# Longer warming products, x tile 0 ahead of W, and the ids product moved behind label 0's work

## The chip, the cores and the metric

The kernel runs on one core of a Trainium2 chip. The metric is the time of one execution on the device in microseconds (us), as the median of several runs. Beside it stands a profile of one further execution: a page and a trace, whose times count from the start of the span (the stretch from the first to the last instruction).

## The reference

Two linear layers with residuals act on `x` of shape 64 x 32 x 512 (batch, sequence, features), all in float32. Cut to what matters:

```python
x = x + einsum('bct,bcd->bdt', x, W0[cond])          # a 32 x 32 mix of each batch's rows, W0 chosen by cond
base  = einsum('bsi,oi->bso', x, W)                  # W is 512 x 512
low   = einsum('bsi,bir->bsr', x, lora_A[label])     # label in 0..2 here, 5 labels of A, rank 32
delta = einsum('bsr,or->bso', low, lora_B_w) * 0.5
x = x + (base + delta)
```

## The kernel before

**The tiling.** A tile is 128 rows of x (four batches of 32), a pair is two tiles; there are 16 tiles in 8 pairs. Since both layers are linear, the kernel applies the second one first: u = x times M, where M = (identity + W transposed + A of label 0 times B), and mixes the rows of u by a block-diagonal matrix (identity + W0 chosen by `cond`) afterwards. Labels other than 0 are handled by the difference of their A to A of label 0 (`a_diff`), whose product with x (`p_low`) is masked by `keep`, folded (`p_fold`) and multiplied with B (`delta_tile`). To keep float32 accuracy with the rounded type fp32r, an operand is split in two, hi (rounded by ScalarE) and lo (the remainder, by VectorE): `xt_hi`/`xt_lo`, `m_hi`/`m_lo`, `ad_hi`/`ad_lo` and so on.

**The five instruction streams.** Each engine has its own list of instructions, written out by hand and worked off strictly in order; semaphores join them. SyncE (SP) issues the loads of W, of x and the stores; ScalarE (ACT) issues three loads first, then copies and rounds; VectorE (DVE) makes remainders and masks; GpSimd (POOL) makes the identity, the indices, the differences of A and the gathers of W0; TensorE (PE) transposes and multiplies.

**The start on TensorE** (lines 637 to 700), in order: seven warming products of a 128 x 128 float32 tile of ones with itself into `p_low` (L639), whose result nothing uses; the transposes of B and A of label 0 (L643); the transposes of W, two quarters (L616); the transposes of x tile 0 into `p_low` (L632); the ids product (`spread_ids`, L650), which spreads `cond` and `label` over 128 partitions into `p_fold`; `lora_half(0)` (L622), which adds A times B to the left half of M; the other two quarters of W; `lora_half(1)`; the transposes of x tile 1 into `p_fold`, behind a wait for the copy of the ids; then `main_tile` for tiles 0 and 1, left half, `main_tile` for tile 0, right half; `low_pair(0)` (L573, L574, and with a wait for `ad_lo` L578); `main_tile` for tile 1, right half; `low_pair(1)`, `fold_pair` (L594, L595); and from there a loop over pairs.

**What hangs on the ids.** DVE copies the ids product out of PSUM (L477, `ids_all`, semaphore `s_ids_sb`). POOL waits for it before it makes the row numbers `w0_row` (L267, four instructions), the mask `keep` (L270), `a_diff` (L276), the gathers of W0 for tiles 0 and 1 (L252) and `ad_lo` (L285), in that order. ACT makes `ad_hi` (L337) from `a_diff`.

**Order on DVE** at the start: memsets; `bw_rep` and `a_rep` (L449 to L457); the identity added to two diagonal blocks of W (L464); `fold_parts`, `fold_to`; the ids to fp32r (L475); the ids' copy (L477), the remainder of x tile 0 (L403), the remainders of the left half of M (L483), and so on. POOL adds the identity to the other two diagonal blocks (L248). Order on ACT: `b_stack` (L327), `a_stack` (L329), x tile 0 rounded (L302), `m_hi` left half (L323), x tile 1 rounded.

Of the kernel before, what the change touches and what calls it, by code (L numbers as in the profile page):

```python
# [27 lines left out]
F32 = mybir.dt.float32  # L28
F32R = mybir.dt.float32r
# [4 lines left out]
P = 128  # L34


def conditioned_lora_kernel(nc, x, cond, label, W0, W, A, Bw, out):
    B, S, T = x.shape
# [6 lines left out]
    OC = O // P  # L45
    Q = P // R
    ROWS = 2 * P
    WARM = 7
    H = O // 2
    W_ORDER = (1, 0, 3, 2)  # L50
    LOOPS = PAIRS // 2 - 1
# [12 lines left out]
    with ExitStack() as ctx:  # L64
        def sb(name, shape, dt=F32):
            return ctx.enter_context(nc.sbuf_tensor(name, shape, dt))
# [5 lines left out]
            return ctx.enter_context(nc.semaphore(name))  # L72


        warm = sb("warm", [P, P])
        ident = sb("ident", [P, P])
        fold_id = sb("fold_id", [P, R])
        fold_parts = sb("fold_parts", [P, 2, 2, 2, R])
# [5 lines left out]
        ids_i = sb("ids_i", [1, 2, B], I32)  # L84
        ids_r = sb("ids_r", [1, 2, B], F32R)
        ones_r = sb("ones_r", [1, P], F32R)
        ids_all = sb("ids_all", [P, 2, B])
        w0_row = sb("w0_row", [P, TILES], I32)
        keep = sb("keep", [P, B])
        w_sb = sb("w_sb", [P, OC, T])  # L90
        a_sb = sb("a_sb", [P, NL, C, R])
        bw_sb = sb("bw_sb", [P, OC, R])
# [29 lines left out]
        p_y = [ps(f"p_y{i}", [P, O]) for i in range(2)]  # L122
        p_low = ps("p_low", [P, O])
        p_fold = ps("p_fold", [P, O])


        s_cond_in = sem("s_cond_in")
# [60 lines left out]
        @blk.sync  # L188
        def _(sp):

            def load(p, slot):

                for q in range(Q):
                    sp.dma_start(x_sb[R * q:R * (q + 1), slot].rearrange("s u b j -> s (u b) j"),
                                 x_pair[p, q]).then_inc(s_x_in[slot], 16)

            def store(p):
                sp.wait_ge(s_y_copied, 2 * p + 2)
                sp.dma_start(out_pair[p], y_sb[:, bass.ds(2 * p, 2)]).then_inc(s_y_out, 16)

            sp.dma_start(bw_sb[:], Bw.rearrange("(o p) r -> p o r", p=P)).then_inc(s_bw_in, 16)
            sp.dma_start(w_sb[:, 0], W[0:P, :]).then_inc(s_w_in[0], 16)
            sp.dma_start(x_rows[:, 0], x_tile[0]).then_inc(s_rows_in[0], 16)
            sp.dma_start(ids_i[:, 0], cond.unsqueeze(0)).then_inc(s_cond_in, 16)
            sp.dma_start(ids_i[:, 1], label.unsqueeze(0)).then_inc(s_label_in, 16)
            sp.dma_start(w_sb[:, 2], W[2 * P:3 * P, :]).then_inc(s_w_in[2], 16)
            sp.dma_start(x_rows[:, 1], x_tile[1]).then_inc(s_rows_in[1], 16)
            sp.dma_start(a_sb[:, 1:NL].rearrange("p l c r -> p l (c r)"), A_cols[:, 1:NL]).then_inc(s_a_in, 16)
            load(1, 1)
            load(2, 0)  # L210

            with sp.Fori(0, LOOPS - 1) as g:
                for slot in (1, 0):
                    sp.wait_ge(s_xt, 2 * (2 * g + 2 - slot))
                    load(2 * g + 4 - slot, slot)
                    store(2 * g + 1 - slot)
            sp.wait_ge(s_xt, 2 * (PAIRS - 3))
            load(PAIRS - 1, 1)
            store(PAIRS - 4)
            store(PAIRS - 3)  # L220
            store(PAIRS - 2)
            sp.wait_ge(s_y_copied, TILES - 1)
            sp.dma_start(out_tile[TILES - 2], y_sb[:, TILES - 2]).then_inc(s_y_out, 16)
            sp.wait_ge(s_last, 2)
            sp.dma_start(out_tile[TILES - 1], y_sb[:, TILES - 1]).then_inc(s_y_out, 16)
            sp.wait_ge(s_y_out, 16 * (PAIRS + 1))
# [65 lines left out]

        @blk.scalar
        def _(act):
            act.dma_start(a_sb[:, 0].rearrange("p c r -> p (c r)"), A_cols[:, 0]).then_inc(s_a0_in, 16)
            act.dma_start(w_sb[:, 1], W[P:2 * P, :]).then_inc(s_w_in[1], 16)
            act.dma_start(w_sb[:, 3], W[3 * P:4 * P, :]).then_inc(s_w_in[3], 16)

            def split_rows(u, bank):

                act.wait_ge(s_rows_t, u + 1)
                nc.scalar.activation(xt_hi[:, 0, :, P * u:P * (u + 1)],  # L302
                                     bank[:].rearrange("p (c r) -> p c r", c=C), COPY).then_inc(s_xhi, 1)
# [16 lines left out]
            def split_m(half, b):  # L320
# [2 lines left out]
                nc.scalar.activation(m_hi[:, 2 * b:2 * b + 2, halves[half]],  # L323
                                     p_u[2 * half + b][:].rearrange("p (c o) -> p c o", c=2), COPY).then_inc(s_mhi, 1)

            act.wait_ge(s_bT, 1)
            nc.scalar.activation(b_stack[:], p_y[0][:], COPY, scale=0.5).then_inc(s_b_stack, 1)  # L327
            act.wait_ge(s_aT, 1)
            nc.scalar.activation(a_stack[:], p_y[1][:], COPY).then_inc(s_a_stack, 1)  # L329
            split_rows(0, p_low)  # L330
            split_m(0, 0)
            split_m(0, 1)
            split_rows(1, p_fold)
# [59 lines left out]
        def _(dve):  # L393
# [5 lines left out]
            def split_rows(u, bank):  # L399

                dve.wait_ge(s_xhi, u + 1)
                cols = slice(P * u, P * (u + 1))
                nc.vector.tensor_tensor(xt_lo[:, 0, :, cols], bank[:].rearrange("p (c r) -> p c r", c=C),  # L403
                                        xt_hi[:, 0, :, cols].bitcast(F32), ALU.subtract).then_inc(s_xlo, 1)
# [26 lines left out]
                                        ALU.subtract).then_inc(s_keptlo, 1)  # L431


            nc.vector.memset(warm[:], 1.0).then_inc(s_warm, 1)
            for j in range(BT):
                nc.vector.memset(group[R * j:R * (j + 1)], float(j)).then_inc(s_group, 1)
            nc.vector.memset(block[:], 0.0).then_inc(s_group, 1)
# [2 lines left out]
            for j in range(BT):  # L440
# [1 line left out]
            dve.wait_ge(s_pool, 1)  # L442
            nc.vector.scalar_tensor_tensor(row_of[:], group[:], -float(R), p_num[:], ALU.mult,
                                           ALU.add).then_inc(s_row_of, 1)
            nc.vector.tensor_copy(ones_r[:], warm[0:1, :]).then_inc(s_ids, 1)

            dve.wait_ge(s_bw_in, 16)
            bw_two = bw_sb[:].unsqueeze(2).broadcast_to([P, OC, 2, R])
# [12 lines left out]
            for o in W_ORDER[:2]:  # L461
                dve.wait_ge(s_w_in[o], 16)
                w_diag = w_sb[:, o, P * o:P * (o + 1)]
                nc.vector.tensor_tensor(w_diag, w_diag, ident[:], ALU.add).then_inc(s_diag, 1)  # L464

            dve.wait_ge(s_pool, 4 + Q)
            for part in range(2):
                nc.vector.tensor_copy(fold_parts[:, part, :, part],
# [4 lines left out]
            dve.wait_ge(s_cond_in, 16)  # L473
            dve.wait_ge(s_label_in, 16)
            nc.vector.tensor_copy(ids_r[:], ids_i[:]).then_inc(s_ids, 1)  # L475
            dve.wait_ge(s_ids_all, 1)
            nc.vector.tensor_copy(ids_all[:].rearrange("p u b -> p (u b)"), p_fold[:, 0:2 * B]).then_inc(s_ids_sb, 1)  # L477

            def split_m(half, b):

                dve.wait_ge(s_mhi, 2 * half + b + 1)
                two, cols = slice(2 * b, 2 * b + 2), halves[half]
                nc.vector.tensor_tensor(m_lo[:, two, cols], p_u[2 * half + b][:].rearrange("p (c o) -> p c o", c=2),  # L483
                                        m_hi[:, two, cols].bitcast(F32), ALU.subtract).then_inc(s_mlo, 1)

            split_rows(0, p_low)
            split_m(0, 0)
            split_m(0, 1)
            split_rows(1, p_fold)
            split_m(1, 0)  # L490
            split_m(1, 1)
# [75 lines left out]
        def _(pe):  # L567
# [13 lines left out]
            def main_tile(bank, slot, u, cols=slice(0, O), half=None):  # L581

                to = bank[:, cols]
                rows = slice(P * u, P * (u + 1))
                for c in range(C):
                    if half is not None:
                        pe.wait_ge(s_mlo, 2 * half + c // 2 + 1)
                    mm(to, xt_hi[:, slot, c, rows], m_hi[:, c, cols], start=(c == 0 and half != 1), stop=False)  # L588
                    mm(to, xt_hi[:, slot, c, rows], m_lo[:, c, cols], start=False, stop=False)  # L589
                    mm(to, xt_lo[:, slot, c, rows], m_hi[:, c, cols], start=False, stop=False)  # L590
# [36 lines left out]
            def transpose_rows(u, bank):  # L627

                pe.wait_ge(s_rows_in[u], 16)
                rows_t = x_rows[:, u].rearrange("p (t c) -> p c t", c=C)  # L630
                for c in range(C):
                    last = mm(bank[:, P * c:P * (c + 1)], rows_t[:, c], ident[:], start=(c == 0), stop=(c == C - 1),  # L632
                              is_transpose=True)
                last.then_inc(s_rows_t, 1)
# [1 line left out]

            pe.wait_ge(s_warm, 1)
            for i in range(WARM):
                mm(p_low[:, 0:P], warm[:], warm[:], start=True, stop=True)  # L639

            def transpose_groups(bank, source):
                for c in range(C):
# [4 lines left out]
            def spread_ids():  # L647

                pe.wait_ge(s_ids, 2)
                mm(p_fold[:, 0:2 * B], ones_r[:], ids_r[:].rearrange("p u b -> p (u b)"), start=True,  # L650
                   stop=True).then_inc(s_ids_all, 1)

            pe.wait_ge(s_pool, 3)
            pe.wait_ge(s_rep, 2)
            transpose_groups(p_y[0], bw_rep).then_inc(s_bT, 1)
            pe.wait_ge(s_rep, 4)
# [2 lines left out]
            transpose_w(0)  # L659
            pe.wait_ge(s_diag, 2)  # L660
            transpose_w(1)
            transpose_rows(0, p_low)
            spread_ids()
            pe.wait_ge(s_b_stack, 1)
            pe.wait_ge(s_a_stack, 1)
            lora_half(0)
# [2 lines left out]
            pe.wait_ge(s_diag_right, 2)  # L669
            transpose_w(3)  # L670
            lora_half(1)
            pe.wait_ge(s_ids_sb, 1)
            transpose_rows(1, p_fold)

            pe.wait_ge(s_xlo, 1)
            main_tile(p_y[0], 0, 0, left, half=0)
            pe.wait_ge(s_xlo, 2)
            main_tile(p_y[1], 0, 1, left, half=0)
            main_tile(p_y[0], 0, 0, right, half=1)
            pe.wait_ge(s_adhi, 1)  # L680
# [76 lines left out]
```

## Time and profile before

| what | value |
|---|---|
| median of 3 runs | 88.50 us (88.23 to 88.61) |
| the profiled execution's own time | 88.51 us |
| its span | 86.7 us |
| PE busy | 82.6 us, 95% of the span |
| DVE busy | 55.8 us, 64% |
| ACT busy | 39.6 us, 46% |
| POOL busy | 23.3 us, 27% |

A difference of two kernels is read on the executions' times; the span leaves out 1.8 us around the instructions. The chain of waits goes back from the last instruction to what released each one; its pieces begin where the piece before them ends, so a piece on PE can start some 0.1 to 0.2 us later than the record of the same product in the timeline, whose records overlap.

### The profile page before, as it was taken

The page shows a single profiled execution, that of the slowest core. Times are in us where ns is not written, and L with a number is a line of the kernel's source. Part 1 is how long each engine was busy: PE and PEld are TensorE (multiplying, and loading weights), DVE is VectorE, ACT ScalarE, POOL GpSimd, SP SyncE. Part 2 cuts the span into 40 slices and gives each one's busy share as a digit, 9 for nine tenths or more (in the row PEclk, how much of TensorE's full clock was granted, in tenths as well). Part 3 has the DMA queues.
Part 4 walks back from the last instruction along what each step waited for, and adds up shares of the span by engine and source line. Part 5 has one row for each costly group of instructions (what it writes and reads, how often), then busy time and mean ns, then how long its engine had stood idle before and what let it go on. Part 6 is the DMA issues. An engine that isn't in the chain of part 4 may idle for free.

```text
span 86.7 us, 1411 instructions
## 1 busy us (share of the span) xinstructions
PE 82.6 (95%) x463; PEld 72.9 (84%) x463; DVE 55.8 (64%) x117; ACT 39.6 (46%) x80; POOL 23.3 (27%) x37
## 2 busy tenths in 40 slices
PE   5999999999999999999999999999999999999950
PEld 5999999998888988898889888988898888889940
DVE  3672879975984696469744984499249933731550
ACT  0544492233547573457255616551754273415440
POOL 5322798977008001800170008000710000000000
PEclk9999999999999999999999999999999999999999
DMA  1999990370000494646037502770250015000606
GB/s 27 314 350 310 199 188 19 83 178 12 8 0 8 147 267 81 203 126 176 2 140 230 134 0 83 230 186 0 80 177 0 0 50 192 8 0 3 239 14 228
DMA packets 12393, 10.16 MB, mean 117 GB/s; under 512 B 1508, under 2 KB 9572, under 8 KB 12388
## 3 DMA queue, kind: packets, MB, share of 16 engines
q1 hardware_dynamic: 11444, 9.24, 38.1%
q10 hardware_dynamic: 432, 0.59, 2.1%
q0 software_dynamic: 512, 0.26, 1.7%
q8 instruction: 3, 0.05, 0.3%
q14 instruction: 2, 0.02, 0.1%
HBM read 5.90 MB, written 4.19 MB: 116 GB/s over the span
## 4 chain that ended last, share of the span: by engine, by line
PE 95%; DVE 1%; issue 0%
PE p_u L588 15%; PE p_u L589 15%; PE p_u L590 15%; PE p_low L573 5%; PE p_low L578 5%; PE p_low L574 4%; PE p_low L639 4%; PE p_u L599 4%; PE p_y L605 4%; PE p_y L606 4%; PE p_y L608 4%; PE p_u L616 3%; PE p_y L588 2%; PE p_y L589 2%; PE p_y L590 2%; PE p_y L643 2%
## 5 line engine op out<-in xcount | busy, mean ns | idle before, releaser
L252 POOL DMA_INDIRECT w_sel<-in_L_cond_weights,w_row x16 | 16.3, 1019 | 33.4 <-DVE diag L499 30.3
L588 PE MATMUL p_u<-m_hi,xt_hi 128*128 128x512 f32 (+1 forms) x60 | 22.6, 377 | 0.0
L589 PE MATMUL p_u<-m_lo,xt_hi 128*128 128x512 f32 (+1 forms) x60 | 22.6, 377 | 0.0
L590 PE MATMUL p_u<-m_hi,xt_lo 128*128 128x512 f32 (+1 forms) x60 | 22.5, 375 | 0.0
L410 DVE TENSOR_TENSOR xt_lo<-xt,xt_hi 128x512 fp32r<-128x512 f32 x14 | 10.1, 728 | 8.4 <-ACT xt_hi L308 8.4
L396 DVE STREAM_TRANSPOSE xt<-x_sb 128x512 f32<-128x512 f32 x14 | 15.1, 1091 | 0.0
L416 DVE TENSOR_TENSOR u_lo<-p_u,u_hi 128x512 fp32r<-128x512 f32 (+1 forms) x15 | 9.3, 652 | 8.9 <-ACT u_hi L313 8.8
L318 ACT ACTIVATE y_sb<-p_y 128x512 f32 (+1 forms) x13 | 7.7, 591 | 12.2 <-PE p_y L608 12.2
L590 PEld LDWEIGHTS p_u<-m_hi,xt_lo 128*128 128x128 f32 x60 | 11.3, 188 | 2.1
L588 PEld LDWEIGHTS p_u<-m_hi,xt_hi 128*128 128x128 f32 x60 | 11.3, 188 | 1.9
L589 PEld LDWEIGHTS p_u<-m_lo,xt_hi 128*128 128x128 f32 x60 | 11.3, 188 | 1.8
L313 ACT ACTIVATE u_hi<-p_u 128x512 fp32r<-128x512 f32 (+1 forms) x15 | 7.8, 568 | 8.7 <-PE p_u L599 8.7
L308 ACT ACTIVATE xt_hi<-xt 128x512 fp32r<-128x512 f32 x14 | 8.8, 632 | 3.9 <-DVE xt L396 1.9
L573 PE MATMUL p_low<-xt_hi,ad_hi 128*128 128x256 f32 x32 | 8.0, 284 | 0.0
L574 PE MATMUL p_low<-xt_lo,ad_hi 128*128 128x256 f32 x32 | 8.0, 283 | 0.0
L341 ACT ACTIVATE kept_hi<-kept 128x256 fp32r<-128x256 f32 x8 | 3.3, 418 | 7.2 <-DVE kept L423 7.2
L573 PEld LDWEIGHTS p_low<-xt_hi,ad_hi 128*128 128x128 f32 x32 | 6.1, 190 | 0.4 <-issue 0.2
L574 PEld LDWEIGHTS p_low<-xt_lo,ad_hi 128*128 128x128 f32 x32 | 6.1, 191 | 0.2
L506 DVE TENSOR_TENSOR diag_lo<-diag,diag_hi 128x256 fp32r<-128x256 f32 x8 | 3.3, 418 | 3.2 <-ACT diag_hi L349 3.2
L605 PE MATMUL p_y<-u_hi,diag_hi 128*128 128x512 f32 (+1 forms) x14 | 5.4, 385 | 0.0
L606 PE MATMUL p_y<-u_hi,diag_lo 128*128 128x512 f32 (+1 forms) x14 | 5.4, 385 | 0.0
L608 PE MATMUL p_y<-u_lo,diag_hi 128*128 128x512 f32 (+1 forms) x14 | 5.3, 381 | 0.0
(92 smaller groups left out, 126.7 us busy)
## 6 DMA issues: line engine op xcount, KB each, us to landing
x_sb<-in_x SPq DMA_DIRECT2D x28, 128.0 KB
out<-y_sb SPq DMA_DIRECT2D x7, 512.0 KB, 3.2
w_sb<-in_L_cond_W ACTq DMA_DIRECT2D x2, 256.0 KB, 3.9
w_sb<-in_L_cond_W SPq DMA_DIRECT2D x2, 256.0 KB, 3.8
x_rows<-in_x SPq DMA_DIRECT2D x2, 256.0 KB, 4.5
out<-y_sb SPq DMA_DIRECT2D x2, 256.0 KB, 2.1
a_sb<-in_L_cond_lora_A SPq DMA_DIRECT2D x1, 256.0 KB, 5.3
w_sel<-in_L_cond_weights,w_row POOLq DMA_INDIRECT x16
```

Source lines behind the costliest of these rows:

```text
L252: nc.gpsimd.indirect_dma_start(out=w0_sel[:, t, :], out_offset=None, in_=W0_rows, in_offset=bass.IndirectOffsetOnAxis(ap=w0_row[:, t:t + 1 ...
L308: nc.scalar.activation(xt_hi[:, slot, :, P * u:P * (u + 1)], xt[:, u], COPY).then_inc(s_xhi, 1)
L396: nc.vector.transpose(xt[:, u].rearrange("p c (b s) -> p c b s", s=S), x_sb[:, slot, u].rearrange("p b (i c) -> p c b i", c=C)).then_inc(s ...
L410: nc.vector.tensor_tensor(xt_lo[:, slot, :, cols], xt[:, u], xt_hi[:, slot, :, cols].bitcast(F32), ALU.subtract).then_inc(s_xlo, 1)
L416: nc.vector.tensor_tensor(u_lo[:, u, cols], bank[:, cols], u_hi[:, u, cols].bitcast(F32), ALU.subtract).then_inc(s_ulo, 1)
L573: mm(p_low[:, 0:ROWS], ad_hi[:, c], xt_hi[:, slot, c], start=(c == 0), stop=False)
L574: mm(p_low[:, 0:ROWS], ad_hi[:, c], xt_lo[:, slot, c], start=False, stop=False)
L588: mm(to, xt_hi[:, slot, c, rows], m_hi[:, c, cols], start=(c == 0 and half != 1), stop=False)
L589: mm(to, xt_hi[:, slot, c, rows], m_lo[:, c, cols], start=False, stop=False)
L590: mm(to, xt_lo[:, slot, c, rows], m_hi[:, c, cols], start=False, stop=False)
L605: mm(to[:, cols], diag_hi[:, slot, u], u_hi[:, u, cols], start=True, stop=False)
L606: mm(to[:, cols], diag_lo[:, slot, u], u_hi[:, u, cols], start=False, stop=False)
```

## The change

The seven warming products become six, of the rounded type and 512 columns wide each. SP issues x tile 0 first and then the four quarters of W in the order in which they are used; Bw, A of label 0 and the ids go on ACT's queue. The transposes of x tile 0 stand in front of B's on PE, and their rounding and remainder stand correspondingly ahead on ACT and DVE. The ids product moves from in front of `lora_half(0)` to behind `lora_half(1)` and writes to `p_y[1]` instead of `p_fold`; its copy on DVE moves behind the remainders of the left half of M; PE waits for that copy before `p_y[1]` is next written.

```diff
-    WARM = 7
+    WARM = 6
-        warm = sb("warm", [P, P])
+        warm = sb("warm", [P, P], F32R)
# SP
-            sp.dma_start(bw_sb[:], Bw.rearrange("(o p) r -> p o r", p=P)).then_inc(s_bw_in, 16)
-            sp.dma_start(w_sb[:, 0], W[0:P, :]).then_inc(s_w_in[0], 16)
             sp.dma_start(x_rows[:, 0], x_tile[0]).then_inc(s_rows_in[0], 16)
-            sp.dma_start(ids_i[:, 0], cond.unsqueeze(0)).then_inc(s_cond_in, 16)
-            sp.dma_start(ids_i[:, 1], label.unsqueeze(0)).then_inc(s_label_in, 16)
-            sp.dma_start(w_sb[:, 2], W[2 * P:3 * P, :]).then_inc(s_w_in[2], 16)
+            for o in W_ORDER:
+                sp.dma_start(w_sb[:, o], W[P * o:P * (o + 1), :]).then_inc(s_w_in[o], 16)
# ACT
+            act.dma_start(bw_sb[:], Bw.rearrange("(o p) r -> p o r", p=P)).then_inc(s_bw_in, 16)
             act.dma_start(a_sb[:, 0].rearrange("p c r -> p (c r)"), A_cols[:, 0]).then_inc(s_a0_in, 16)
-            act.dma_start(w_sb[:, 1], W[P:2 * P, :]).then_inc(s_w_in[1], 16)
-            act.dma_start(w_sb[:, 3], W[3 * P:4 * P, :]).then_inc(s_w_in[3], 16)
+            act.dma_start(ids_i[:, 0], cond.unsqueeze(0)).then_inc(s_cond_in, 16)
+            act.dma_start(ids_i[:, 1], label.unsqueeze(0)).then_inc(s_label_in, 16)
+            split_rows(0, p_low)
             act.wait_ge(s_bT, 1)
...
-            split_rows(0, p_low)
             split_m(0, 0)
# DVE
+            split_rows(0, p_low)
             dve.wait_ge(s_pool, 4 + Q)
...
-            dve.wait_ge(s_ids_all, 1)
-            nc.vector.tensor_copy(ids_all[:]..., p_fold[:, 0:2 * B]).then_inc(s_ids_sb, 1)
-            split_rows(0, p_low)
             split_m(0, 0)
             split_m(0, 1)
+            dve.wait_ge(s_ids_all, 1)
+            nc.vector.tensor_copy(ids_all[:]..., p_y[1][:, 0:2 * B]).then_inc(s_ids_sb, 1)
             split_rows(1, p_fold)
# PE
-                mm(p_low[:, 0:P], warm[:], warm[:], start=True, stop=True)
+                mm(p_low[:], warm[:], warm[:].unsqueeze(1).broadcast_to([P, 4, P]), start=True, stop=True)
-                mm(p_fold[:, 0:2 * B], ones_r[:], ids_r[:]..., start=True,
+                mm(p_y[1][:, 0:2 * B], ones_r[:], ids_r[:]..., start=True,
             pe.wait_ge(s_pool, 3)
+            transpose_rows(0, p_low)
             pe.wait_ge(s_rep, 2)
...
-            transpose_rows(0, p_low)
-            spread_ids()
             pe.wait_ge(s_b_stack, 1)
             pe.wait_ge(s_a_stack, 1)
             lora_half(0)
...
             lora_half(1)
-            pe.wait_ge(s_ids_sb, 1)
+            spread_ids()
             transpose_rows(1, p_fold)
             pe.wait_ge(s_xlo, 1)
             main_tile(p_y[0], 0, 0, left, half=0)
             pe.wait_ge(s_xlo, 2)
+            pe.wait_ge(s_ids_sb, 1)
             main_tile(p_y[1], 0, 1, left, half=0)
```

## Rows read from the trace of the kernel before

**Rows 1.** The page: busy time of each engine; granted clock of PE in 40 slices.

```profile
PE 82.6 (95%) x463; PEld 72.9 (84%) x463; DVE 55.8 (64%) x117; ACT 39.6 (46%) x80; POOL 23.3 (27%) x37
...
PEclk9999999999999999999999999999999999999999
```

**Rows 2.** Chain of waits, from the start (start us, us, engine tile line).

```profile
1.06 3.36 PE p_low L639 x14
4.41 1.71 PE p_y L643 x8
6.12 1.24 PE p_u L616 x8
7.36 0.48 PE p_low L632 x4
7.84 0.25 PE p_fold L650
8.09 0.68 PE p_u L622 x4
8.77 0.96 PE p_u L616 x8
9.73 0.47 PE p_u L622 x4
10.20 0.49 PE p_fold L632 x4
```

**Rows 3.** Chain of waits, around the first two low_pair.

```profile
16.21 0.67 PE p_low L578 x4
...
18.32 0.35 PE p_low L573
...
19.98 0.12 PE p_fold L594
...
20.22 0.23 PE p_u L588
```

**Rows 4.** Timeline of POOL (start us, us, instruction, [idle before]).

```profile
7.09 0.46 POOL L248 TENSOR_TENSOR w_sb<-w_sb,ident 128x128 f32<-128x128 f32 x1 [0.58 <-DMA w_sb<-in_L_cond_W]
8.71 1.43 POOL L267 TENSOR_SCALAR w_row<-ids_all,row_of 32x16 int32<-32x16 f32 x4 [1.16 <-DVE ids_all L477]
...
10.84 1.30 POOL L276 TENSOR_TENSOR a_diff<-a_sb 128x512 f32<-128x512 f32 x1
...
13.79 0.95 POOL L252 DMA_INDIRECT w_sel<-in_L_cond_weights,w_row  x1 [0.30 <-issue]
14.77 1.31 POOL L285 TENSOR_TENSOR ad_lo<-a_diff,ad_hi 128x512 fp32r<-128x512 f32 x1
```

**Rows 5.** Timeline of DVE.

```profile
4.17 0.43 DVE L457 TENSOR_TENSOR a_rep<-a_sb,a_rep 128x256 fp32r<-128x256 f32 x1
...
8.13 0.29 DVE L477 COPY ids_all<-p_fold 128x128 f32<-128x128 f32 x1 [1.54 <-PE p_fold L650]
...
9.19 1.29 DVE L483 TENSOR_TENSOR m_lo<-p_u,m_hi 128x512 fp32r<-128x512 f32 x2
...
17.16 0.21 DVE L496 TENSOR_TENSOR mix<-w_sel,fold_id 128x64 f32<-128x64 f32 x1
...
17.75 0.42 DVE L423 TENSOR_TENSOR kept<-p_low,keep 128x256 f32<-128x256 f32 x1
```

**Rows 6.** Timeline of ACT.

```profile
6.16 0.60 ACT L329 ACTIVATE a_stack<-p_y 128x512 fp32r<-128x512 f32 x1 [0.26 <-PE p_y L643]
...
12.18 0.64 ACT L337 ACTIVATE ad_hi<-a_diff 128x512 fp32r<-128x512 f32 x1
```

**Rows 7.** The page: GB/s in 40 slices; a DMA issue (us to landing last).

```profile
GB/s 27 314 350 310 199 188 19 83 178 12 8 0 8 147 267 81 203 126 176 2 140 230 134 0 83 230 186 0 80 177 0 0 50 192 8 0 3 239 14 228
...
x_rows<-in_x SPq DMA_DIRECT2D x2, 256.0 KB, 4.5
```

**Rows 8.** Timeline of SP's queue.

```profile
0.74 0.44 SPq L201 DMA_DIRECT2D bw_sb<-in_L_cond_lora_B_w  x1
```

More of the change, by code:

```diff
@@ L431, in split_low @@
                                         ALU.subtract).then_inc(s_keptlo, 1)
-            nc.vector.memset(warm[:], 1.0).then_inc(s_warm, 1)
+            nc.vector.memset(warm[:].bitcast(F32), 1.0).then_inc(s_warm, 1)
             for j in range(BT):
@@ L444, in _ @@
                                            ALU.add).then_inc(s_row_of, 1)
-            nc.vector.tensor_copy(ones_r[:], warm[0:1, :]).then_inc(s_ids, 1)
+            nc.vector.tensor_copy(ones_r[:], warm[0:1, :].bitcast(F32)).then_inc(s_ids, 1)
             dve.wait_ge(s_bw_in, 16)
@@ L475, in _ @@
             nc.vector.tensor_copy(ids_r[:], ids_i[:]).then_inc(s_ids, 1)
-            dve.wait_ge(s_ids_all, 1)
-            nc.vector.tensor_copy(ids_all[:].rearrange("p u b -> p (u b)"), p_fold[:, 0:2 * B]).then_inc(s_ids_sb, 1)
             def split_m(half, b):
@@ L484, in split_m @@
                                         m_hi[:, two, cols].bitcast(F32), ALU.subtract).then_inc(s_mlo, 1)
-            split_rows(0, p_low)
             split_m(0, 0)
             split_m(0, 1)
+            dve.wait_ge(s_ids_all, 1)
+            nc.vector.tensor_copy(ids_all[:].rearrange("p u b -> p (u b)"), p_y[1][:, 0:2 * B]).then_inc(s_ids_sb, 1)
             split_rows(1, p_fold)
@@ L649, in spread_ids @@
                 pe.wait_ge(s_ids, 2)
-                mm(p_fold[:, 0:2 * B], ones_r[:], ids_r[:].rearrange("p u b -> p (u b)"), start=True,
+                mm(p_y[1][:, 0:2 * B], ones_r[:], ids_r[:].rearrange("p u b -> p (u b)"), start=True,
                    stop=True).then_inc(s_ids_all, 1)
             pe.wait_ge(s_pool, 3)
+            transpose_rows(0, p_low)
             pe.wait_ge(s_rep, 2)
```

## The prediction

> **What bounds the kernel now.** I read the page first: PE is busy 95% of the span, DVE 64% [rows 1], so the time is PE's queue plus the moments in which it waits. The chain of waits comes next, because it says whether that queue is ever released by somebody else. In the first 10.7 us it is PE alone, piece on piece from 1.06 us on [rows 2]: warming, B and A, W, x tile 0, the ids, and so on. So the start is bound by PE too, and each of its microseconds counts.
>
> The pieces also show PE's two speeds. Eight transposes of B and A take 1.71 us, 0.213 each; eight of W (the second group) take 0.96, 0.12 each [rows 2]. The group between takes 1.24 for eight: with n of them at 0.213 and 8 - n at 0.12 that is n = 3, so the speed changed at 6.12 + 3 x 0.213 = 6.76 us. The page's clock line stands at its top digit throughout and does not show this [rows 1]; 256 columns' worth of streaming in 0.213 us is the 1.2 GHz level, and 0.12 goes with 2.4 GHz. What PE did before the change of speed was to work without a pause since 1.06 us.
>
> Then I looked for the places in which PE is released by others, later than the start. Two stand out [rows 3]: four products of L578 take 0.67 us where four at 0.12 would take 0.48, so 0.19 is waiting; and one product of L573 takes 0.35, so 0.23 is waiting. The timelines say for whom. POOL ends `ad_lo` at 14.77 + 1.31 = 16.08 [rows 4], just where L578 begins. And POOL is busy up to there almost without a break from 8.71 us, where it was released by DVE's copy of the ids; that copy ended at 8.13 + 0.29 = 8.42 [rows 4, 5] and was itself released by the ids product, which ends at 8.09 [rows 2]. So a second chain, ids product to copy to POOL's row numbers, mask, `a_diff`, two gathers and `ad_lo`, runs beside PE's queue and meets it at L578 with no slack (PE waited 0.19). Its length is 16.21 + 0.67 - 8.09 = 8.79 us from the end of the ids product to the end of L578's block. This is the fact on which my forecast rests. The L573 wait is for `kept` (DVE ends it at 18.17, [rows 5]).
>
> **The change part by part.** All in the times of the chain.
>
> *Warming.* A float32 product of 128 columns appears as two records; 14 records take 3.36 us [rows 2], which is 14 x 0.213 = 2.98 and 0.38 for the first to come through. No row shows a rounded 512-column product at the slow level. At the fast level one takes 0.23 [rows 3]; times 0.213/0.12 that is 0.41, times two 0.46, and 512 columns at 1.2 GHz are 0.427. I take 0.427, as the slow rows follow columns over clock exactly (256 columns, 0.213). Six make 2.56, with 0.38 in front 2.94, so warming ends at 4.00 instead of 4.41: 0.41 earlier (bounds 0.22 for 0.46, 0.52 for 0.41).
>
> *x tile 0 first.* Its load now goes first, at about 0.74 us [rows 8], with 64 KB of Bw and 64 KB of A beside it on the other queue. By the GB/s line 58 KB had moved at 2.17 us and 314 GB/s x 2.17 us = 681 KB more by 4.33 [rows 7], so the first 384 KB are through at about 3.2 us. PE wants it at 4.00. The bound from the other side is the 4.5 us from issue to landing that this tile took in third place [rows 7]: 5.24, which would hold PE for 1.24 us at the slow level. I take the first, since nothing stands before it; cost nothing, covered by the warming products. The four transposes now run at 0.213 (0.85 us) instead of 0.48 in all, and W's eight then start at 4.00 + 0.85 + 1.71 = 6.56. If the speed still changes at 6.76, one of them is slow and seven fast: 0.20 + 0.84 = 1.04, end at 7.60. Seen otherwise: of 0.41 us of slow work saved, 0.41 x 0.12/0.213, about 0.24, remains once the clock is up.
>
> *`lora_half(0)`* started at 8.09 and now can at 7.60: 0.24 from the above, 0.25 because the ids product no longer stands before it. It needs `a_stack`. That followed A's last transpose directly (6.12 in the chain, started 6.16, 0.60 long, [rows 2, 6]), so it ends at about 6.56 + 0.04 + 0.60 = 7.20. Before it ACT now rounds x tile 0 (end about 5.5) and then makes `b_stack` (about 6.35). Cover 0.4 us; nothing added.
>
> *The loads of W and A, Bw and ids on ACT's queue.* W's last two blocks are wanted at 8.28 and 8.76; POOL had the last ready at 7.09 + 0.46 = 7.55 with W in a longer queue [rows 4]. A later landing by up to 0.7 us would be hidden. ACT issues four loads instead of three, roughly 0.4 us more, against a first use at 4.9. SP issues one fewer before x's tiles. Bw and A feed transposes that now come 0.4 us later. All at nothing; if several covers failed together it would be some 0.3 us.
>
> *The ids product moved.* It now follows `lora_half(1)`: 7.60 + 0.68 + 0.96 + 0.47 + 0.25 = 9.96 us at its end, instead of 8.09: 1.87 later. For PE's queue alone it is neutral; the main products start at 10.69 - 0.24 = 10.45. Its copy on DVE stands behind the two remainders of M. Those ended at 10.48 [rows 5]; `lora_half(0)` comes 0.49 earlier and the remainder of x tile 0 is out of the way, so they end at about 9.9 and DVE waits for PE or the reverse by under 0.1. The copy ends about 10.29 and POOL starts its row numbers at 8.71 + 1.87 = 10.58.
>
> *What is late next.* POOL has no slack to take this up: row numbers, mask, `a_diff`, gathers, `ad_lo` follow each other. `a_diff` ends at 12.14 + 1.87 = 14.01, ACT makes `ad_hi` by 14.7 [rows 4, 6], and PE wants it at about 15.0: just hidden; rounding of tile 2 behind it on ACT is not hurt by more than 0.3. `ad_lo` ends at 17.95, and L578's block at 16.88 + 1.87 = 18.75. PE arrives at it at 16.21 - 0.24 = 15.97, needs 0.48, and so stands idle for 2.30 us. Behind that wait stand, in PE's order, tile 1's right half, `low_pair(1)` and all the rest.
>
> *A little comes back.* Tile 1's right half ends at 18.32 + 1.87 = 20.19. `kept` waits in DVE's order behind the mix of gathered rows. In the kernel before, gather 1 was issued until 14.74 and its rows were in use at 17.16 [rows 4, 5], so it landed in 2.42 us or less; now 16.61 + 2.42 = 19.03, plus 1.01 for mix to `kept` (17.16 to 18.17), 20.04. That is in time, so the wait of 0.23 at L573 goes (or stays: bounds 0 and 0.23). Sum: +1.87 - 0.23 = **+1.64 us**. From there on the pieces on PE follow each other as before. On the profiled execution's time: 88.51 + 1.64 = 90.15; the median of the runs is 88.50, so I forecast **90.1 us**.
>
> **The rivals.**
>
> *A. The speed changes earlier, and the change is no slower.* The place is PE before the ids product; what decides is when that product ends. At 8.09 + 0.23 = 8.32 the loss is zero, at 8.76 it is the 0.44 us that are 0.5%. If the fast level stood at 4.00, when the warming ends, x, B, A and W would be 0.48, 0.48, 0.48, 0.96 (`a_rep` is ready at 4.60 [rows 5], in time), reaching 6.40; `lora_half(0)` to 7.08, W to 8.04 (the last block is ready by 7.55), `lora_half(1)` 8.51, ids 8.76. That gives +0.67 - 0.23 = +0.44, 88.9, and less if some warming products were fast as well, about 88.6. For it: wider products leave fewer gaps. Against it: the slow rows already stream at 1.2 GHz without gaps, so PE is no busier than before.
>
> *B. The speed changes later.* The warming is 0.41 shorter and twelve instead of eight transposes follow it. If the slow level lasted to the ids product, W's first eight take 1.71 (+0.67), the next eight +0.75, the eight products of `lora_half` (0.213 each for 256 columns, 1.70 for 1.15) +0.55, the ids product +0.1: +2.1, 92.2; if it lasted half that way, about 91.2. Against it: in the kernel before the speed rose amid transposes [rows 2]. In the Trainium skill, "TensorE: Matmul & The Clock Gate", Part 4, it says that the fast level does not engage for transposes, which don't count as work of PE. By that rule what comes after the warming could not raise the clock, and B would be the likely case; the trace speaks against its strict form, as the rise fell 2.35 us after the last warming product.
>
> *C. The clock falls in the idle 2.30 us.* Then the 28 products of 256 columns behind it (4, 12 and 12) could take 0.213 for 0.12: +2.6, 92.7. No row has such a pause; the longest after the start is 0.23.
>
> *D. The ids chain doesn't decide*, and only PE's 0.24 is left: 88.3. Against it: L578 waited for `ad_lo` already.
>
> **How the numbers follow.** Forecast 0.64, by itself 89.7 to 90.5 (bounds of warming, half of x's lateness, the 0.23); A 0.14; B 0.10; C 0.05; D 0.04; something else 0.03. The range 88.8 to 91.4 leaves out C, D, most of B's dearer half and of A's cheap end, under 2 in 10. Within 0.5% (0.44 us, what a measurement here can tell from no change) lie most of A and part of D: 0.15; faster 0.04; slower 0.81.
>
> **What would show it.** In the profile after: warming ends near 4.0; x's transposes follow with no wait; W's first group near 6.56, with about one slow transpose; the ids product ends near 10.0; POOL's row numbers start near 10.6; L578's block ends near 18.75 after an idle PE of over 2 us, put down to POOL's `ad_lo`; L573's wait is gone. I am wrong if the ids product ends before 8.8, or if POOL's pieces between ids and `ad_lo` get shorter.

## The result, and the profile after

The changed kernel took 91.56 us (median of 4 executions, 90.71 to 93.8) against 88.56 (88.23 to 88.64): ratio 1.0335, 95% interval 1.029 to 1.0381. I had forecast 90.1 with a range to 91.4, so the direction and the place were right and the size was not: +3.0 where I had +1.6. The profiled execution took 91.40 us with a span of 89.5, 2.8 more than before. Three of the four executions had a slow stretch of TensorE that the forecast left out (below); the fourth took 90.71 us, which lies inside my range.

The page and the chain of waits of the changed kernel, the lines that answer to [rows 1 to 3]:

```profile
PE 83.4 (93%) x455; PEld 72.4 (81%) x455; DVE 55.5 (62%) x117; ACT 39.7 (44%) x80; POOL 23.0 (26%) x37
...
PEclk9999999975999999999999999999999999999999
```

```profile
1.06 2.93 PE p_low L637 x6
3.98 0.89 PE p_low L630 x4
4.88 0.81 PE p_y L641 x4
...
5.70 0.65 PE p_y L641 x4
6.35 0.96 PE p_u L614 x8
...
9.58 0.30 DVE ids_all L486
...
10.15 0.29 POOL w_row L264
...
12.29 1.30 POOL a_diff L273
...
16.33 1.29 POOL ad_lo L282
...
17.67 0.75 PE p_low L576 x4
18.41 0.12 PE p_y L586
...
19.15 0.21 PE p_y L586
...
20.43 0.21 PE p_low L571
...
22.14 0.65 PE p_low L576 x4
22.78 0.11 PE p_fold L592
23.01 0.23 PE p_u L586
```

Before, this chain was PE alone; now it leaves PE at the rounding of M (ACT at 7.64, then DVE's remainders) and comes back at 17.67 with the `ad_lo` products (L576, L578 before). That is the second chain that I had described, now the longer one. The end of that block moved from 16.88 to 18.41: **+1.53 us**. Then something follows that the sum didn't hold: from 19.15 on the products of 256 columns are 0.21 apart, not 0.12, until 22.78. From 18.41 to the fold product are 4.37 us; before, from 16.88 to 19.98, 3.10: **+1.27 us**. The 0.23 us wait of [rows 3] is gone in this, so the slow stretch itself costs 1.50: six products of the main tile, eight of L571 and L572, and about two of the four of L576, some 16 in all, each 0.09 us longer. 1.53 + 1.27 = 2.80 is the whole difference of the spans.

The granted clock in windows of the same trace (us from the start; length; busy time of PE, PE's weight loads, DVE, ACT and POOL; PEclk; DMA share; GB/s):

```profile
18.50:19.00 0.50, 0.50 (x7) 0.50 (x6) 0.45 (x2) 0.38 (x2) 0.24 (x1) 0.97 0.89 197
19.00:20.00 1.00, 1.00 (x7) 1.00 (x6) 0.57 (x2) 0.40 (x2) 0.95 (x1) 0.50 0.29 68
20.00:21.00 1.00, 1.00 (x7) 1.00 (x6) 0.19 (x1) 0.00 (x0) 0.70 (x1) 0.50 0.06 14
21.00:22.00 1.00, 1.00 (x7) 1.00 (x6) 0.00 (x0) 0.00 (x0) 0.70 (x2) 0.50 0.03 9
22.00:23.00 1.00, 1.00 (x8) 1.00 (x8) 0.11 (x1) 0.00 (x0) 0.49 (x1) 0.81 0.06 9
23.00:24.00 1.00, 1.00 (x6) 0.79 (x5) 0.52 (x2) 0.72 (x2) 0.00 (x0) 1.00 0.08 16
```

0.50 is the 1.2 GHz level. PE had idled 1.95 us before, worked again for about 1.3 us, and then, at about 19.0 us, the clock fell although PE was fully busy. It was back at about 22.4 (0.81 in the window from 22 to 23). The timelines show the idle time and its releaser, and POOL's wait that answers to [rows 4]:

```profile
17.67 0.75 PE L576 MATMUL p_low<-xt_hi,ad_lo 128*128 128x256 f32 x4 [1.95 <-POOL ad_lo L282]
```

```profile
10.15 1.43 POOL L264 TENSOR_SCALAR w_row<-ids_all,row_of 32x16 int32<-32x16 f32 x4 [2.52 <-DVE ids_all L486]
```

### The profile page after: what moved, and what is told of

The parts are those of the page before. It is cut to its first block, busy times and chain, and to the rows that moved or that the text cites. A ratio compares the mean times of both kernels' runs of the same rounds, so it can differ in the third digit from the quotient of the medians.

```text
span 89.5 us, 1394 instructions
## 1 busy us (share of the span) xinstructions
PE 83.4 (93%) x455; PEld 72.4 (81%) x455; DVE 55.5 (62%) x117; ACT 39.7 (44%) x80; POOL 23.0 (26%) x37
## 4 chain that ended last, share of the span: by engine, by line
PE 84%; POOL 7%; DVE 3%; issue 2%; ACT 1%; POOLq 0%
PE p_u L586 14%; PE p_u L587 14%; PE p_u L588 14%; PE p_low L576 5%; PE p_low L572 4%; PE p_low L571 4%; PE p_u L597 4%; PE p_y L603 3%; PE p_y L604 3%; PE p_y L606 3%; PE p_low L637 3%; POOL w_sel L249 2%; PE p_y L641 2%; POOL a_diff L273 1%; POOL ad_lo L282 1%
## 5 line engine op out<-in xcount | busy, mean ns | idle before, releaser
L408 DVE TENSOR_TENSOR xt_lo<-xt,xt_hi 128x512 fp32r<-128x512 f32 x14 | 9.5, 680 | 8.4 <-ACT xt_hi L306 8.4
L572 PE MATMUL p_low<-xt_lo,ad_hi 128*128 128x256 f32 x32 | 8.7, 299 | 0.0
L571 PE MATMUL p_low<-xt_hi,ad_hi 128*128 128x256 f32 x32 | 8.6, 298 | 0.0
L576 PE MATMUL p_low<-xt_hi,ad_lo 128*128 128x256 f32 x32 | 5.5, 294 | 1.9 <-POOL ad_lo L282 1.9
L572 PEld LDWEIGHTS p_low<-xt_lo,ad_hi 128*128 128x128 f32 x32 | 6.7, 208 | 0.2
L571 PEld LDWEIGHTS p_low<-xt_hi,ad_hi 128*128 128x128 f32 x32 | 6.6, 208 | 0.2
L576 PEld LDWEIGHTS p_low<-xt_hi,ad_lo 128*128 128x128 f32 x32 | 4.7, 204 | 2.1 <-POOL ad_lo L282 2.1
```

The source lines that it names most:

```text
L408: nc.vector.tensor_tensor(xt_lo[:, slot, :, cols], xt[:, u], xt_hi[:, slot, :, cols].bitcast(F32), ALU.subtract).then_inc(s_xlo, 1)
L571: mm(p_low[:, 0:ROWS], ad_hi[:, c], xt_hi[:, slot, c], start=(c == 0), stop=False)
L572: mm(p_low[:, 0:ROWS], ad_hi[:, c], xt_lo[:, slot, c], start=False, stop=False)
L576: last = mm(p_low[:, 0:ROWS], ad_lo[:, c], xt_hi[:, slot, c], start=False, stop=(c == C - 1))
```

## The experiments

Times are medians; behind them stand the ratio to the kernel before on the same chip and its 95% interval (an estimate of its own, so it need not be the quotient of the two medians). "Clock" is the mean granted clock of an execution; the two profiled executions with a slow stretch as above have 0.981, and I count every execution at 0.980 or 0.981 as one that had it. All others have 0.994 or more. Each experiment has one profile, so what is read from a trace holds for that execution.

**1. The ids product back in its place, the rest of the change kept.**

```diff
             transpose_w(1)
+            spread_ids()
...
             lora_half(1)
-            spread_ids()
+            pe.wait_ge(s_ids_sb, 1)
```

> The changed kernel with one part undone: the ids product stands in front of lora_half(0) again and its copy where it was on DVE; warming, x tile 0 first and the queues stay changed. Theory (the moved ids product starts POOL's chain late, PE stands idle at ad_lo, and the idle lets the clock fall): both terms go, PE is some 0.3 us ahead of the kernel before, 88.0 to 88.5 us, granted clock 1.00 in every stretch, no wait at the ad_lo products over 0.3 us. Rival 1 (the new order of loads and the shorter warming cost the time): it stays at 91 or so. Rival 2 (the clock falls because of the warming, whatever the wait): the clock falls as in the changed kernel, about 90.

88.84 us, 1.0041 (1.0013 to 1.007), no execution of 12 below clock 0.994. The large loss is gone, so it hangs on the ids move. But I had expected the kernel to be ahead of the kernel before, 88.0 to 88.5, and it is not; the timeline of PE shows a wait.

```profile
5.62 0.66 PE L641 MATMUL p_y<-ident,a_rep 128*128 128x128 f32 x4 [0.22 <-DVE a_rep L455]
...
8.33 0.32 PE L648 MATMUL p_fold<-ids_r,ones_r 1*128 1x128 f32 x1 [1.00 <-DVE ids_r L474]
```

PE waits 1.00 us for DVE to convert the ids, an instruction that the change left behind x tile 0's remainder and the fold tiles. Experiment 12 tests whether that is the reason.

**2. The ids product moved, nothing else.** The kernel before with `spread_ids()` behind `lora_half(1)`, into `p_y[1]`, and its copy behind the left half's remainders.

> The kernel before with one part of the change alone: the ids product behind lora_half(1), into p_y[1], with its copy behind the left half's remainders. Theory: the ids product ends about 1.9 us later than before, the ad_lo products end about 1.9 later, PE idles about 2.0 us there; +1.6 us by the wait and +1.5 us if the clock falls in it, 91 to 92. Rival 1 (loads and warming cost it): within 0.5 of before. Rival 2 (the clock falls only with the new warming): about 90.1, clock 1.00 throughout.

91.18 us, 1.0321 (1.0273 to 1.037): as much as the whole change, with the old warming and the old loads. PE waited 2.14 us:

```profile
18.95 0.74 PE L578 MATMUL p_low<-xt_hi,ad_lo 128*128 128x256 f32 x4 [2.14 <-POOL ad_lo L285]
```

Three of six executions have a clock of 0.98 (91.31, 92.01, 92.63 us), three 0.996 or more (90.70, 90.92, 91.04). The fall is thus a matter neither of the new warming nor of the new loads. In the profile (the execution of 92.63 us) the clock fell about 1.6 us after PE was back at work. The pause part is larger here than in the changed kernel: the ids product ended at 10.60 us, 2.51 later than before where I had expected 1.9, as x tile 0 landed late (PE waited 0.25) and POOL had the last block of W ready at 8.66 instead of 7.55. These loads are those of the kernel before; they landed later in this execution.

**3 and 4. PE kept at work in the wait.** Products of ones go in front of the wait for `ad_lo`, seven in one kernel and three in the other; their result is not used.

```diff
                 if waits:
+                    for i in range(7):
+                        mm(p_u[0][:], warm[:], warm[:].unsqueeze(1).broadcast_to([P, 4, P]), start=True, stop=True)
                     pe.wait_ge(s_adlo, 1)
```

> The changed kernel with seven added products of ones (512 columns, result unused, into the bank p_u[0] that is free there) between the hi products of low_pair(0) and the wait for ad_lo, so that PE works through most of its idle 1.9 us. Theory (wait and clock are two terms, and idleness is what lowers the clock): the ad_lo products still end at 18.4 us, the clock stays at 1.00, and the 17 products that took 0.21 us for 0.12 take 0.12: about 1.6 less than the changed kernel's profiled 91.4, 89.8 us. Rival (the clock falls for another reason, or the added work delays PE): 91.4 or more.

> The changed kernel with three added products of ones instead of e3_fill's seven, so that PE idles about 1.2 us of the 1.9. Theory (idleness in that wait lowers the clock, in the more executions the longer it is): fewer executions near clock 0.98 than the changed kernel's six of ten, 0 to 2 of 6; those at 1.00 take about 90.3. Rival (any pause does it, or the products' place): half or more of the executions near 0.98.

90.47 us (1.0212, 1.0168 to 1.0255) with seven, 90.14 (1.0219, 1.0185 to 1.0253) with three. The idle time is 0.31 and 1.21 us instead of 1.95, and none of the twelve executions has a clock below 0.997.

```profile
16.70 1.78 PE L575 MATMUL p_u<-warm 128*128 128x512 f32 x7
18.79 0.74 PE L578 MATMUL p_low<-xt_hi,ad_lo 128*128 128x256 f32 x4 [0.31 <-POOL ad_lo L282]
```

```profile
17.68 0.74 PE L578 MATMUL p_low<-xt_hi,ad_lo 128*128 128x256 f32 x4 [1.21 <-POOL ad_lo L282]
```

Work that nobody uses makes the kernel faster than the changed one by about a microsecond (by the ratios about 0.01), and what is gone is the slow stretch: with the fillers it takes about what the changed kernel takes in the executions that keep their clock (90.46, experiment 5). The kernel with three ran on another chip than the one with seven and than experiments 2 and 5; that chips differ in how readily the clock falls is not ruled out for it. With seven it missed my 89.8. In the profiled execution, at 90.94 us the longest of the six, A of label 0 landed 4.75 us after its issue on ACT's queue, `a_rep` started at 6.01, and PE waited 1.08 us for it; the `ad_lo` products began at 18.79, not 17.67. What kept the others above 89.8 (two of them took 89.76 and 89.81) is not shown.

**5. The changed kernel again.**

> The changed kernel itself again, on the chip of the other runs of this call. Theory (wait for ad_lo, Bw and A landing late, and in most executions a fall of the clock in or after the wait): 90.7 to 92, executions with a mean granted clock near 0.98 longer by 0.5 to 1.6 us than those at 1.00. Rival (the length doesn't go with the clock): no such order among the executions.

90.93 us, 1.0312 (1.0257 to 1.0368). With the four executions of the result there are ten: clock 0.98 in six, 91.38, 91.40, 91.72, 91.72, 91.73 and 93.80 us, and 0.999 or 1.000 in four, 89.92, 90.43, 90.49 and 90.71. The medians are 91.72 and 90.46, so the fall costs about 1.3 us where it comes. The profiled execution here is one at 0.999 (89.92 us), and PE idled just as long in it, 1.92 us (the first row is of the timeline, the second of the chain):

```profile
17.78 0.74 PE L576 MATMUL p_low<-xt_hi,ad_lo 128*128 128x256 f32 x4 [1.92 <-POOL ad_lo L282]
...
20.92 0.48 PE p_low L576 x4
```

So such a pause can be followed by a fall of the clock and isn't always. The two profiles of the same kernel also price the fall. From the end of the first `ad_lo` block to the fold product this one takes 21.40 - 18.52 = 2.88 us, the other 4.37: 1.49 us.

**6. `a_diff` in front of POOL's wait for the ids.**

```diff
+            pool.wait_ge(s_a0_in, 16)
+            pool.wait_ge(s_a_in, 16)
+            nc.gpsimd.tensor_tensor(a_diff[:], ...).then_inc(s_adiff, 1)
             pool.wait_ge(s_group, BT)
             pool.wait_ge(s_row_of, 1)
             pool.wait_ge(s_ids_sb, 1)
```

> The changed kernel with one instruction moved on POOL: a_diff, which needs no ids, stands in front of the wait for the ids, in time in which POOL idled 2.5 us. Everything else stays, the late ids product too. Theory: row numbers to ad_lo becomes 1.3 to 1.4 us shorter, ad_lo ends about 16.3 instead of 17.6, PE waits about 0.5 us instead of 1.9, the clock holds: 88.4 to 88.9. Rival (the gathers or kept decide instead, not ad_lo): PE waits as long at the next low_pair, 90 or more.

89.21 us, 1.0101 (1.0049 to 1.0153); a clock of 0.98 in one of six. One instruction moved on POOL gives back most of the loss with the ids product left late; the wait for `ad_lo` is 0.60 us in the profile. The execution with the fall took 91.12 us and has no trace, so how long PE paused in it is not known. The median ended above my range, 88.4 to 88.9. In the profile the rest of A landed at 9.25, 5.67 us after its issue, so `a_diff` ended at 10.66 and itself held POOL a little, and the ids product ended at 10.00 instead of 9.54, as the fast clock came later.

**7. The loads alone.** The kernel before with the change's DMA issues and nothing else.

> The kernel before with the DMA issues of the change alone: x tile 0 and W on SP, Bw, A of label 0 and the ids on ACT; all engines compute in the old order with the old warming. Theory (Bw and A land 0.8 us or more later on ACT's queue beside 256 KB loads, and this is a third, small and scattered term): bw_rep starts at about 4.0 us instead of 3.1, a_rep at 4.8 to 6.0, PE waits 0.3 to 1.5 us at the transposes of B and A, the ids product comes that much later: +0.3 to +0.8 us, with more spread over executions than before. Rival (the loads are hidden, as I had predicted): within 0.2 us of before.

88.67 us, 1.003 (1.0009 to 1.0051): 0.2 to 0.3 us, just under the 0.3 to 0.8 that I had expected. Bw landed 3.2 us after its issue in the changed kernel, 2.4 before, and PE waited here before the first transpose:

```profile
4.85 1.09 PE L641 MATMUL p_y<-ident,bw_rep 128*128 128x128 f32 x4 [0.45 <-DVE bw_rep L449]
```

**8. The warming alone.** The kernel before with six rounded products of 512 columns.

> The kernel before with the warming products of the change alone: six rounded ones of 512 columns instead of seven float32 ones of 128. Theory (the warming ends 0.4 us earlier, of which 0.24 remains once the clock is up; B is ready just in time): 0.1 to 0.3 us faster than before, fast level at 6 to 6.8 us. Rival (wider products change when the clock rises): the rise at another time by a microsecond or more, and the total moves by over 0.4 us either way.

88.53 us, 1.0004 (0.9973 to 1.0034): no gain, where I had expected 0.1 to 0.3 us. PE's timeline:

```profile
1.05 2.93 PE L639 MATMUL p_low<-warm 128*128 128x512 f32 x6 [1.05 <-DVE warm L434]
4.38 0.63 PE L643 MATMUL p_y<-ident,bw_rep 128*128 128x128 f32 x4 [0.41 <-DVE bw_rep L451]
4.96 0.66 PE L643 MATMUL p_y<-ident,a_rep 128*128 128x128 f32 x4
6.13 1.23 PE L616 MATMUL p_u<-ident,w_sb 128*128 128x128 f32 x8 [0.51 <-DVE w_sb L464]
...
7.77 0.32 PE L650 MATMUL p_fold<-ids_r,ones_r 1*128 1x128 f32 x1
```

The warming ends 0.4 us earlier and the transposes of B are fast at once, but PE then waits 0.41 for B and 0.51 for W, and the ids product starts at 7.77 us, as in the profile of before (there 7.84 in the chain, which counts from the end of the product before). What PE saves in the warming it spends waiting for loads.

**9. The ids earlier instead of later.** Six warming products, the ids loaded second on SP's queue, their product in front of x tile 0's transposes.

> The opposite of the change: the kernel before with the six wider warming products, the ids loaded second on SP's queue, behind Bw, and the ids product one step earlier on PE, in front of the transposes of x tile 0. Theory (the ids chain to ad_lo is what meets PE, so starting it earlier takes its waits away): POOL's row numbers start about 0.5 us earlier, the waits of 0.19 at the ad_lo products and 0.23 at the next low_pair go, with 0.24 from the warming: 87.7 to 88.1. Rival (those waits come back elsewhere, or the later W and x loads hold PE): 88.3 or more.

88.36 us, 0.9995 (0.9976 to 1.0014): no gain, where I had expected 87.7 to 88.1. Both waits went, the 0.19 us at the `ad_lo` products wholly and the 0.23 at the next low_pair but for 0.05 (first row; 0.28 would be without a wait). PE lost nearly as much at the start: it waited 0.32 us for B, and of W's first eight transposes four to five were still slow (second row, from the chain), so the fast level came at about 7.2 us instead of 6.8 and the main products began at 10.95 instead of 10.69.

```profile
18.22 0.33 PE L573 MATMUL p_low<-xt_hi,ad_hi 128*128 128x256 f32 x1
...
6.24 1.37 PE p_u L616 x8
```

Nor did POOL's row numbers start half a microsecond earlier. They started at 8.60 instead of 8.71, behind the identity's addition to W's last block, which landed later.

**10 and 11. Bw and A first in their queues,** in the kernels of experiments 1 and 6:

```diff
+            sp.dma_start(bw_sb[:], Bw.rearrange("(o p) r -> p o r", p=P)).then_inc(s_bw_in, 16)
             sp.dma_start(x_rows[:, 0], x_tile[0]).then_inc(s_rows_in[0], 16)
# ACT
-            act.dma_start(bw_sb[:], Bw.rearrange("(o p) r -> p o r", p=P)).then_inc(s_bw_in, 16)
```

> e1_ids_back (the changed kernel with the ids product back in front of lora_half(0)) with Bw loaded first on SP's queue, ahead of x tile 0, and A of label 0 first on ACT's, as both were before. Theory (what e1_ids_back lost against my sum is Bw and A landing late): bw_rep starts near 3.2 us instead of 3.9, a_rep near 3.9 instead of 4.8, PE no longer waits for a_rep, total 88.2 to 88.6. Rival (it is W or the order on DVE that holds the ids product): bw_rep and a_rep come early but the ids product doesn't, 88.8 as e1_ids_back.

> e4_adiff_first (the changed kernel, late ids product kept, a_diff in front of the wait for the ids) with the same two loads put first. Theory (terms add up): about 0.3 us less than e4_adiff_first's 89.2, 88.7 to 89.1. Rival (after a_diff is moved the chain from the ids decides alone and the loads don't matter): 89.2.

Both missed, and both theories with them: 89.63 us (1.0112, 1.0068 to 1.0155) and 90.46 (1.0201, 1.0152 to 1.0249). Neither is faster than the kernel it was made from; both medians are higher, though their intervals just touch those of experiments 1 and 6. B came early (`bw_rep` at 3.05 in the first), but x tile 0, now issued 0.5 us later, was late:

```profile
5.45 0.72 PE L630 MATMUL p_low<-ident,x_rows 128*128 128x128 f32 x4 [1.47 <-DMA x_rows<-in_x]
```

That is the second kernel's profile; in the first's the wait was 0.37. The lateness had moved to what PE wants first. In the second kernel another late load decided, though: SP issued the rest of A 0.58 us later than in experiment 6, it landed at about 10.0 us, and `a_diff`, now ahead of the row numbers, held POOL until 11.38 (10.66 in experiment 6):

```profile
10.12 1.27 POOL L258 TENSOR_TENSOR a_diff<-a_sb 128x512 f32<-128x512 f32 x1 [1.43 <-DMA a_sb<-in_L_cond_lora_A]
11.38 1.43 POOL L270 TENSOR_SCALAR w_row<-ids_all,row_of 32x16 int32<-32x16 f32 x4
```

The `ad_lo` block ended 0.72 us later than in experiment 6's profile (18.25, 17.53), which accounts for the difference of the two profiled executions (89.88, 89.17). PE paused 1.47 and 0.98 us in this kernel, and none of its six executions has a clock below 0.994. Why the first kernel's median is 89.63 its profile can't say: the profiled execution, at 88.86, is one of the two shortest.

**12. Experiment 1 with DVE's order mended.** The ids are converted behind W's diagonal blocks and copied ahead of the fold tiles.

> e1_ids_back with DVE's order mended: the ids are converted right behind W's two diagonal blocks and copied ahead of fold_parts and fold_to, so that they no longer stand behind x tile 0's remainder and the fold tiles. Theory (in e1_ids_back PE waited 1.00 us for the converted ids, and that wait, not the loads as such, is its loss): the wait falls to 0.3 us or less, POOL's row numbers start near 8.5 instead of 9.3, total 88.1 to 88.4, the kernel before or slightly under it. Rival (W landing late holds PE anyway): 88.8 as e1_ids_back.

88.33 us, 0.9975 (0.9948 to 1.0001), as expected. The 1.00 us wait is gone, so it was the loss of experiment 1, and no execution is below clock 1.000.

```profile
7.48 0.32 PE L648 MATMUL p_fold<-ids_r,ones_r 1*128 1x128 f32 x1
```

So everything in the change but the ids move, with DVE's order fitted to it, is worth at most half a per cent, and the interval reaches to nothing. No version clearly beats the kernel before. Of the 66 executions of experiments 1, 7, 8, 9, 10 (the first kernel) and 12, none has a clock of 0.98; in their profiles PE never waited more than 0.3 us for `ad_lo`.

## Why the prediction was wrong

**Right: what bounds the kernel.** The ids chain took over at the `ad_lo` products. Experiment 2 shows that the ids move by itself makes a loss as large as the whole, 6 that shortening POOL's chain gives most of it back.

**Right, by steps.** Warming ended at 3.98 (forecast 4.00). x tile 0 was there without a wait (it landed at about 3.6, not 3.2, 0.3 us before PE wanted it). POOL's row numbers started at 10.15 (10.58), the `ad_lo` block ended at 18.41 (18.75), PE idled 1.95 (2.30), and the 0.23 wait went. The chain was 0.4 us better than the sum because the clock rose earlier, by the chain at about 6.1 us instead of 6.76: the second four transposes after x's take 0.65 and W's eight 0.96. That made the ids product end at 9.54 instead of 9.96, and DVE was through with the remainders of M at 9.57, just in time for the copy. Rival A's mechanism was there in part, and the 0.4 us is its effect.

**Wrong: "C. The clock falls in the idle 2.30 us", chance 0.05.** This is the step that failed: the forecast of 90.1 let the clock hold through the pause, for no better reason than that no row had such a pause. The fall came in six of ten executions of the changed kernel, three of six with the ids move alone, and none of twelve when PE worked through part of the pause. Its price was 1.50 us in the profiled execution (some 16 slow products, and the fast level back before the fold), not the 2.6 that I had bounded for 28. It should have had a chance of about a half; with it the range would have reached to 92.7. The four executions of the changed kernel at a clock of 0.999 or more took 89.92 to 90.71 us, 90.46 at the median: all lie inside my range, and my sum was right for them to 0.4 us.

**Wrong in size: the small terms.** I had put the loads at nothing; alone they cost 0.3%, 0.27 us (experiment 7). I had put the warming at -0.24; alone it gave 0.00 (experiment 8), since B and W land no earlier. Inside the changed kernel neither shows as a loss: the one traced execution that kept its clock took 89.92 us, 1.41 more than the profiled one before, against my 1.64. Where the other three have their further 0.5 to 0.8 us no trace shows. Experiment 2, with the old loads and the old warming, has 90.70 to 91.04 for its executions of this kind, so the two terms are not needed for it; loads that land at different times from one execution to the next would do it, which is argued, not shown.

**Rival B** (the clock rises later) did not happen in the changed kernel: its two profiles have the rise at about 6.1 and 6.4 us, the kernel before at 6.8. Of the other kernels' profiles experiment 9's has it clearly later, at about 7.2. The changed kernel's rise came amid transposes again, at about 6.1 us, 2.1 us after the last warming product; in experiment 9's it was 3.2 us. The Trainium skill, "TensorE: Matmul & The Clock Gate", Part 4, says that transposes don't bring the fast level; these traces do not agree with it as it stands.

The runs show falls of the clock behind pauses of 1.95 and 2.14 us. The Trainium skill, "TensorE: Matmul & The Clock Gate", section "Why this matters for your kernels", advises against idle gaps of TensorE of over about 3 us; as a safe length that is too generous for this kernel.

What stays open is what decides between two executions with the same pause (1.95 us with a fall, 1.92 without), and from what length on it happens: in the kernel whose profile has 1.21 us it did not in six, in the one whose profile has 0.60 (experiment 6) it did in one of six, with a pause that no trace shows.

## What to carry to other kernels

Moving an instruction that is cheap on its own engine is priced on the chain that starts from it: add up what other engines do, in order, from its result to the next place where the busy engine meets them. Here the product costs PE 0.25 us wherever it stands, while the 7.7 us of POOL's work behind its copy (8.42 to 16.08) had no slack. A new pause of a microsecond or two on TensorE is to be priced twice, once as the pause and once, with a real chance, as a slow stretch behind it. And time saved by warming less, or by putting one load first, is only real if what comes next has landed.

## What was not expected of the hardware

The clock fell after PE had gone back to full work, by about 1.3 us in the changed kernel and 1.6 in experiment 2's, not in the pause. With the same warming products its rise came at different times: the transposes of B ran fast from 4.38 us in experiment 8's profile, and slowly (1.09 us for four, from 4.30) in experiment 9's. The 64 KB load of A of label 0 took 3.6 to 4.75 us from issue to landing where it stood behind Bw's 64 KB on ACT's queue, and 1.9 to 2.1 where it stood first on that queue.
